# The last chain passes of 35 weight tiles carry the tile's scale, and two sums of token halves go to GpSimd

## The chip, the cores and the metric

One core of a Trainium2 chip runs the kernel. The metric is device time in microseconds (us), the median of three runs.

## The reference

The input x has 2048 tokens (4 x 512) of 512 features. It is normalised over the features, and three terms are added: x itself, a convolution along the features whose kernel comes from a small state-space model (S4), and a gated feed-forward layer with 4-bit weights. Cut to what matters:

```
def dequant_nf4(q, absmax, shape):
    w = NF4_CODE[q.reshape(-1)]
    w = w.reshape(-1, BLOCK) * absmax[:, None]
    return w.reshape(shape)
...
g = jnp.einsum('bsh,mh->bsm', x, Wg)        # M = 1792, HD = 512
u = jnp.einsum('bsh,mh->bsm', x, Wu)
h = jax.nn.silu(g) * u
return jnp.einsum('bsm,hm->bsh', h, Wd)
...
xn = _layernorm(x, axis=-1)
x = x + _L0_attn_ref(xn, ...) + _L0_ffn_ref(xn, ...)
```

## The kernel before, in words

Nothing is scheduled by a tool: each engine has its instructions written out in order, and semaphores tie them together. All large products are computed with float16 operands, and for accuracy each operand is the sum of a high and a low half, so every product is three matmuls (high-high, high-low, low-high).

**Weights.** The 42 weight tiles ("units" u: 14 each of gate, up and down, 128x512) arrive as int32 codes. GpSimd makes a first clamp of the codes (`first_pass`, L846). ScalarE then runs six Prelu passes, three on a left and three on a right chain (`chain_pass`, L937, tags l0 to r2). VectorE joins the chains (`step` WHOLE, L1310) and multiplies by the block's absmax (`step` SCALED, L1314). The high half, scaled by a power of two that stands in the tile `sc`, is made by ScalarE for units 0 to 6 and by GpSimd for the 35 units from 7 on (`weight_hi`, L859); VectorE makes the low half (`weight_lo`, L1324). For gate tiles GpSimd also keeps a scaled float32 copy (`gate_copy`, L868).

**Products.** From weight row k = 3 on, gate and up products are blocked by a Strassen-like scheme with seven products in place of eight: they need sums of weight blocks (`up_sums`, `other_sums`, split into halves by `block_hi` L1058 on ScalarE and `block_lo` L1370 and L1373 on VectorE) and sums of token blocks. The token sums start from high plus low halves of the normalised, transposed tokens `xT`: `token_whole` (L1385, eight of them, two sets s of four), then `token_sum` (L1396), ScalarE's `token_hi` and VectorE's `token_lo` (L1401). Each row k is a "window" in which TensorE runs 14 such products (`blocked_product`, L2270, six matmuls each); ScalarE moves partial results between banks (`copy_m1` L1030, `copy_m5` L1034) and makes silu (L1021), VectorE adds them (`join`, L1413) and multiplies (`h_mul`, L1439). After the windows come the convolution (L2337) and the down projection (L2347, L2397).

**Order around the change.** On GpSimd: `first_pass` of a unit, then layernorm rows (`norm`, L750), `first_pass(8)`, seventeen tiny steps of an exponential (L760 to L776), then a loop over the units from 7 on with `first_pass(u + 2)`, `weight_hi(u)`, `gate_copy(u)`. On VectorE the two sums `token_whole(1, 2)` and `token_whole(1, 3)` follow `step(8, SCALED)`, and `weight_lo(7)` comes later, just ahead of the first blocked window's sums. On ScalarE each window runs the chain passes of two or three units in a fixed place between bank copies and silu, and `block_hi` of the next row last.

Of the kernel before, what the change touches and what calls it, by code (L numbers as in the profile page):

```python
# [6 lines left out]
P = 128  # L7
# [102 lines left out]
]  # L110
CHAIN_TOP, CHAIN_STEP = 0.15385548770427704, 0.5004680156707764
CHAIN_ORDER = ("l0", "r0", "l1", "r1", "l2", "r2")
SIDES_ORDER = ("l0", "l1", "l2", "r0", "r1", "r2")
# [107 lines left out]
def ffn_conv_kernel(nc, x, q_gate, q_up, q_down, am_gate, am_up, am_down, am_flat, s4_cols, vct, bp,  # L221
# [5 lines left out]
    with ExitStack() as ctx:  # L227
# [17 lines left out]
        ident_h = ident[:].bitcast(F16)  # L245
        sc = sb("sc", [P, 34], F32)
        ones = sb("ones", [3, P], F32)
# [179 lines left out]
        def scale_of(u):  # L427
            return s_w[2 if SEQ[u] >= GU else SEQ[u] % 2]

        def whole_of(u):  # L430
            if u in CHAINED:
                return acc[:, (u - CHAINED[0]) % 3, :]
            return acc_1[:, 2, :]
# [51 lines left out]
        wlo_done = sem("wlo_done")  # L485
        sc_done = sem("sc_done")
        mx_tp = sem("mx_tp")
        mx_bc = sem("mx_bc")
# [17 lines left out]
        whs_lo = sem("whs_lo")  # L506
        xb_done = [sem(f"xb_done{s}") for s in range(2)]
        xs_done = [sem(f"xs_done{s}") for s in range(2)]
        xs_hi = [sem(f"xs_hi{s}") for s in range(2)]
# [226 lines left out]
        def _(pool):  # L736
# [112 lines left out]
            def weight_hi(u):  # L849

                pool.wait_ge(dq_done, dq_after(u, SCALED))
                unit = SEQ[u]
                if unit < GU:
                    before = room_before(unit // 2)
                    if LAST_USE[before] is not None:
                        pool.wait_ge((gate_done, up_done)[unit % 2], WHOLE_COUNT[LAST_USE[before]])
                    for s in sides(before):
                        pool.wait_ge(m_done[s], m_at(s, before, (2, 4)[unit % 2]))
                pool.tensor_scalar(weight_of(u)[HI], whole_of(u), scale_of(u), None, ALU.mult).then_inc(phi_done, 1)  # L859

# [51 lines left out]
        def _(act):  # L912
# [10 lines left out]
            def chain_pass(u, j):  # L923
# [123 lines left out]
            def block_hi(k, part):  # L1047
# [5 lines left out]
                elif n >= 2:  # L1053
                    for s in sides(k - 2):
# [225 lines left out]
        def _(dve):  # L1280
            v = nc.vector

            def step(u, s):
# [8 lines left out]
                elif s == WHOLE:  # L1292
# [11 lines left out]
                    if before < GU and before // 2 in BLOCKED:  # L1304
# [3 lines left out]
                        else:  # L1308
                            dve.wait_ge(w_done, 4 * blocked(before // 2) + 2)
                    ins = v.scalar_tensor_tensor(whole, left, CHAIN_TOP if u in CHAINED else LEFT_TOP, right, ALU.min, ALU.add)  # L1310
                else:
                    dve.wait_ge(am_ld[u % 2], 32 * (u // 2 + 1))
                    dve.wait_ge(dq_done, dq_after(u, WHOLE))
                    ins = v.scalar_tensor_tensor(whole, whole, CHAIN_STEP if u in CHAINED else -LEFT_TOP, am[:, u % 2, :],  # L1314
                                                 ALU.add, ALU.mult)
                ins.then_inc(dq_done, 1)

            def weight_lo(u):
# [20 lines left out]
            def up_sums(k, u):  # L1339

                n = blocked(k)
                whole, scale = whole_of(u), scale_of(u)
                g_whole, w_sums = sums_room(k)
                if n:
# [4 lines left out]
                dve.wait_ge(g_done, n + 1)  # L1349
                v.scalar_tensor_tensor(w_sums[:, 2, :], whole[:, 0:FH], scale, g_whole[:, 0:FH],  # L1350
                                       ALU.mult, ALU.subtract).then_inc(w_done, 1)

            def other_sums(k):
# [3 lines left out]
                dve.wait_ge(w_done, 4 * n + 1)  # L1357
                v.scalar_tensor_tensor(w_sums[:, 1, :], w_sums[:, 0, :], s_w[1], g_whole[:, 0:FH],
                                       ALU.mult, ALU.subtract).then_inc(w_done, 1)
                dve.wait_ge(w_done, 4 * n + 3)  # L1360
                v.tensor_tensor(w_sums[:, 3, :], g_whole[:, FH:HD], w_sums[:, 1, :], ALU.subtract).then_inc(w_done, 1)

            def block_lo(k, part):
# [4 lines left out]
                hi, lo = (sums_split(k, first, last)[:, :, l].rearrange("p i f m -> p i (f m)") for l in (HI, LO))  # L1368
                if part == 0:
                    v.scalar_tensor_tensor(lo, w_sums[:, first:last, :], s_w[1], hi,  # L1370
                                           ALU.mult, ALU.subtract).then_inc(whs_lo, 1)
                else:
                    v.tensor_tensor(lo, w_sums[:, first:last, :], hi, ALU.subtract).then_inc(whs_lo, 1)  # L1373

            def token_whole(s, i):

                c, f = (ROLE_E, ROLE_B)[i % 2][s], 2 * (i // 2)
                if s == 0 and f == 0:
                    dve.wait_ge(xt_ld[c - 2], 16 * TPC)
                elif s == 1 and i == 2:  # L1380
                    dve.wait_ge(xp_done, NT - POOL_NORMS)
                elif s == 1 and i == 0:
# [5 lines left out]
            def token_sum(s, i):  # L1388

                b12, b11, b22, b21 = x_sums[s]  # L1390
                if i == 0:
                    dve.wait_ge(xb_done[s], 4)
                else:
# [1077 lines left out]
```

## Time and profile before

| | |
|---|---|
| median of 3 runs | 455.39 us (454.79 to 456.29) |
| the profiled execution, its own time | 455.8 us |
| its span from the first to the last instruction | 454.0 us |
| TensorE busy | 439.6 us, 97% |
| VectorE busy | 397.2 us, 87% |
| ScalarE busy | 279.4 us, 62% |
| GpSimd busy | 214.7 us, 47% |
| mean granted TensorE clock | 0.996 |

The busy times overlap, so they don't add up to the span. TensorE's busy time is modelled from pipelined matmuls; whether it runs without holes is better read from when its products start.

### The profile page before, as it was taken

The page shows a single profiled execution, that of the slowest core. Times are in us where ns is not written, and L with a number is a line of the kernel's source. Part 1 is how long each engine was busy: PE and PEld are TensorE (multiplying, and loading weights), DVE is VectorE, ACT ScalarE, POOL GpSimd, SP SyncE. Part 2 cuts the span into 40 slices and gives each one's busy share as a digit, 9 for nine tenths or more (in the row PEclk, how much of TensorE's full clock was granted, in tenths as well). Part 3 has the DMA queues.
Part 4 walks back from the last instruction along what each step waited for, and adds up shares of the span by engine and source line. Part 5 has one row for each costly group of instructions (what it writes and reads, how often), then busy time and mean ns, then how long its engine had stood idle before and what let it go on. Part 6 is the DMA issues. An engine that isn't in the chain of part 4 may idle for free.

```text
span 454.0 us, 7272 instructions
## 1 busy us (share of the span) xinstructions
PE 439.6 (97%) x2560; PEld 251.6 (55%) x2560; DVE 397.2 (87%) x641; ACT 279.4 (62%) x472; POOL 214.7 (47%) x163
## 2 busy tenths in 40 slices
PE   1989999999999999999999999999999999999997
PEld 1744444444444444444444444466444788888886
DVE  5988979969889798999997779879996999999993
ACT  7878594395887859778675686855032643445340
POOL 2776299544956849769547757687100000000000
PEclk9989999999999999999999999999999999999999
DMA  8534636031415416336212243268790021101111
GB/s 301 163 131 145 157 71 176 1 92 46 164 48 185 162 48 208 113 120 209 71 47 71 60 126 78 86 212 252 212 361 31 17 79 48 46 1 48 48 48 46
DMA packets 34168, 51.41 MB, mean 113 GB/s; under 512 B 13076, under 2 KB 14164, under 8 KB 33364
## 3 DMA queue, kind: packets, MB, share of 16 engines
q1 hardware_dynamic: 34132, 50.95, 35.8%
q8 instruction: 20, 0.33, 0.3%
q14 instruction: 16, 0.13, 0.1%
HBM read 38.03 MB, written 10.81 MB: 108 GB/s over the span
## 4 chain that ended last, share of the span: by engine, by line
PE 91%; DVE 4%; DMA 2%; ACT 1%; issue 1%; POOL 1%; SPq 0%; DVEq 0%; POOLq 0%; ACTq 0%
PE bank L2270 38%; PE bank L2397 21%; PE bank L2115 17%; PE bank L2347 8%; PE bank L2337 6%; DMA h<-in_x 1%; DMA work<-in_q_gate 1%; PE bank L2151 0%; DVE work L1310 0%; DVE work L1314 0%; DVE at_s L1800 0%; POOL h L846 0%; PE bank L2207 0%; ACT xT L1096 0%; DVE w L1324 0%
## 5 line engine op out<-in xcount | busy, mean ns | idle before, releaser
L937 ACT ACTIVATE work<-work 128x512 f32<-128x512 f32 (+1 forms) x234 | 129.9, 625 | 11.5 <-POOL work L846 8.0
L846 POOL TENSOR_SCALAR work<-work 128x512 f32<-128x512 int32 x39 | 83.6, 2143 | 63.0 <-DVE work L1310 42.3
L2270 PE MATMUL bank<-h 128*128 128x512 f16 x360 | 81.4, 379 | 0.0
L2115 PE MATMUL bank<-xT,w 128*128 128x512 f16 (+1 forms) x300 | 66.2, 378 | 0.4 <-ACT yv L1124 0.4
L2270 PEld LDWEIGHTS bank<-h 128*128 128x128 f16 x360 | 35.1, 98 | 42.7 <-ACT bank L1030 0.7
L2397 PE MATMUL bank<-wd,work 128*128 128x256 f16 x504 | 56.2, 273 | 0.0
L2270 PE MATMUL bank<-xT,w 128*128 128x512 f16 x240 | 55.4, 379 | 0.0
L2397 PEld LDWEIGHTS bank<-wd,work 128*128 128x128 f16 (+1 forms) x504 | 49.3, 98 | 6.0
L2115 PEld LDWEIGHTS bank<-xT,w 128*128 128x128 f16 x300 | 30.0, 100 | 34.2 <-issue 1.6
L859 POOL TENSOR_SCALAR w<-work,sc 128x512 f16<-128x512 f32 x21 | 43.6, 2077 | 6.0 <-DVE work L1314 5.0
L1251 ACT ACTIVATE work<-h 128x896 f16<-128x896 f32 x30 | 27.9, 943 | 28.4 <-DVE h L2023 18.3
L2397 PE MATMUL bank<-h,work 128*128 128x256 f16 x378 | 42.2, 273 | 0.0
L2397 PEld LDWEIGHTS bank<-h,work 128*128 128x128 f16 x378 | 37.0, 98 | 4.3
L2270 PEld LDWEIGHTS bank<-xT,w 128*128 128x128 f16 x240 | 23.4, 98 | 28.1
L2347 PE MATMUL bank<-wd,h 128*128 128x512 f16 x168 | 36.4, 379 | 0.0
L2009 DVE TENSOR_TENSOR work<-h,work 128x896 bf16<-128x896 f32 x30 | 32.5, 1083 | 0.1
L1310 DVE SCALAR_TENSOR_TENSOR work<-work 128x512 f32<-128x512 f32 x39 | 27.5, 705 | 4.8 <-ACT work L937 4.8
L1021 ACT ACTIVATE work<-bank,sc 128x512 f32<-128x512 f32 x36 | 24.5, 681 | 10.8 <-PE bank L2115 10.8
L1314 DVE SCALAR_TENSOR_TENSOR work<-work 128x512 f32<-128x512 f32 x41 | 29.3, 714 | 1.1
L2270 PE MATMUL bank<-xT,h 128*128 128x512 f16 x120 | 27.9, 379 | 0.2 <-DVE bank L1413 0.2
L2270 PE MATMUL bank<-h,w 128*128 128x512 f16 x120 | 27.8, 379 | 0.0
L859 POOL TENSOR_SCALAR wd<-work,sc 128x512 f16<-128x512 f32 x14 | 25.5, 1821 | 4.5 <-PE bank L2337 2.5
(181 smaller groups left out, 659.7 us busy)
## 6 DMA issues: line engine op xcount, KB each, us to landing
moved<-h SPq DMA_DIRECT2D x6, 1024.0 KB, 4.9
h<-moved SPq DMA_DIRECT2D x4, 1536.0 KB, 16.5
h<-in_x SPq DMA_DIRECT2D x8, 512.0 KB, 5.2
xT<-in_x SPq DMA_DIRECT2D x16, 256.0 KB, 3.4
out<-xT SPq DMA_DIRECT2D x15, 256.0 KB, 2.1
work<-in_q_gate SPq DMA_DIRECT2D x14, 256.0 KB, 3.7
work<-in_q_up SPq DMA_DIRECT2D x14, 256.0 KB, 2.8
work<-in_am_gate SPq DMA_DIRECT2D x28, 128.0 KB, 3.0
```

Of the source, the lines that this page charges most:

```text
L846: pool.tensor_scalar(chain_room(u, "r"), qs[:, u % 2, :], RIGHT_FROM, RIGHT_FROM, ALU.max, ALU.subtract).then_inc(first_done, 1)
L859: pool.tensor_scalar(weight_of(u)[HI], whole_of(u), scale_of(u), None, ALU.mult).then_inc(phi_done, 1)
L937: nc.scalar.activation(room, qs[:, u % 2, :] if j == 0 else room, KNEE, scale=scale, bias=bias, alpha=below).then_inc(knee_done, 1)
L1251: nc.scalar.activation(slot_of(o)[:, HI], src, ACT.Copy).then_inc(o_hi, 1)
L1310: ins = v.scalar_tensor_tensor(whole, left, CHAIN_TOP if u in CHAINED else LEFT_TOP, right, ALU.min, ALU.add)
L1314: ins = v.scalar_tensor_tensor(whole, whole, CHAIN_STEP if u in CHAINED else -LEFT_TOP, am[:, u % 2, :], ALU.add, ALU.mult)
L2009: v.tensor_tensor(slot[:, LO].bitcast(BF16), src, slot[:, HI], ALU.subtract).then_inc(o_lo, 1)
L2115: mm = nc.tensor.matmul(out_b, weights(k)[:, unit, wl, f, :], xT[:, TPC * c + first:TPC * c + last, xl, f, :], start=(i == 0), stop=(i == ...
L2270: mm = nc.tensor.matmul(out_b, weight(wl, f), token(xl, f), start=(n == 0 and i in (1, 5)), stop=(n == 5), skip_group_check=i not in (1, 5))
L2337: mm = nc.tensor.matmul(bank[(t + 4) % 8][:, P * j:HD], xT[:, t, xl, j, :], tz[:, tl, 0:HD - P * j], start=(n == 0), stop=(n == 3 * NC - 1))
L2347: mm = nc.tensor.matmul(bank[(t + 4) % 8][:], part, wd[:, mt, wl, :], start=(mt == 0 and n == 0), stop=(mt == NM - 1 and n == 2))
L2397: mm = nc.tensor.matmul(out_b, part, w, start=(n == 0), stop=(n == 3 * KT - 1))
```

## The change

The scale of a unit from 7 on is no longer applied where the high half is made. It is folded into the constants of the chain: GpSimd computes six small rows once (`fold`, products of the three scales with six constants, into 18 new columns of `sc`). The last left pass and the last right pass on ScalarE then read scale and bias from `sc` instead of immediates, and the two steps on VectorE read their added constant from `sc`. Since the whole weight is then already scaled, `weight_hi` and `gate_copy` on GpSimd become plain copies, and `weight_lo`, the weight sums and `block_hi` part 0 lose their scale operand. Apart from that, `token_whole(1, 2)` and `token_whole(1, 3)` leave VectorE and are made by GpSimd, each as two instructions of 512 elements, behind the exponential's steps.

```diff
@@ gpsimd
-                pool.tensor_scalar(weight_of(u)[HI], whole_of(u), scale_of(u), None, ALU.mult).then_inc(phi_done, 1)
+                pool.tensor_copy(weight_of(u)[HI], whole_of(u)).then_inc(phi_done, 1)
...
-                pool.tensor_scalar(sums_room(SEQ[u] // 2)[0], whole_of(u), scale_of(u), None, ALU.mult).then_inc(g_done, 1)
+                pool.tensor_copy(sums_room(SEQ[u] // 2)[0], whole_of(u)).then_inc(g_done, 1)
+
+            def fold(i):
+
+                pool.wait_ge(sc_done, WEIGHT_SCALES)
+                pool.tensor_scalar(sc[:, 34 + 3 * i:37 + 3 * i], sc[:, 9:12], FOLDED[i], None, ALU.mult).then_inc(fold_done, 1)
+
+            def token_whole(i):
+
+                c = (ROLE_E, ROLE_B)[i % 2][1]
+                if i == 2:
+                    pool.wait_ge(xlo_done, NT)
...
+                hi, lo = (xT[:, TPC * c:TPC * c + TPC, l, 2:4, :] for l in (HI, LO))
+                made = x_sums[1][i].rearrange("p (f t m) -> p t f m", f=2, t=TPC)
+                for f in range(2):
+                    ins = pool.tensor_tensor(made[:, :, f], hi[:, :, f], lo[:, :, f], ALU.add)
+                ins.then_inc(xbp_done, 1)
...
             first_pass(7)
+            for i in range(len(FOLDED)):
+                fold(i)
...
             for i in range(EXP_STEPS):
                 exp_step(i)
+            token_whole(2)
+            token_whole(3)
@@ scalar
                 scale, bias, below = (RIGHT_CHAIN if side == "r" else LEFT_CHAIN)[i]
+                if u in POOL_HALVES and i == 2:
+                    act.wait_ge(fold_done, len(FOLDED))
+                    at = FOLD_RIGHT if side == "r" else FOLD_LEFT
+                    scale, bias = folded(u, at), folded(u, at + 1)
...
-                                     w_sums[:, first:last, :], ACT.Copy,
-                                     scale=1.0 if part else s_w[1]).then_inc(whs_hi, 1)
+                                     w_sums[:, first:last, :], ACT.Copy).then_inc(whs_hi, 1)
@@ vector
-                    ins = v.scalar_tensor_tensor(whole, left, CHAIN_TOP if u in CHAINED else LEFT_TOP, right, ALU.min, ALU.add)
+                    top = folded(u, FOLD_TOP) if u in POOL_HALVES else CHAIN_TOP if u in CHAINED else LEFT_TOP
...
+                    ins = v.scalar_tensor_tensor(whole, left, top, right, ALU.min, ALU.add)
...
-                v.scalar_tensor_tensor(lo, whole_of(u), scale_of(u), hi, ALU.mult, ALU.subtract).then_inc(wlo_done, 1)
+                if u in POOL_HALVES:
+                    v.tensor_tensor(lo, whole_of(u), hi, ALU.subtract).then_inc(wlo_done, 1)
...
-                v.scalar_tensor_tensor(w_sums[:, 1, :], w_sums[:, 0, :], s_w[1], g_whole[:, 0:FH],
-                                       ALU.mult, ALU.subtract).then_inc(w_done, 1)
+                v.tensor_tensor(w_sums[:, 1, :], w_sums[:, 0, :], g_whole[:, 0:FH], ALU.subtract).then_inc(w_done, 1)
...
             step(8, SCALED)
-            token_whole(1, 2)
-            token_whole(1, 3)
             h_mul(7)
```

Two places of the program's order matter. The first is GpSimd's queue between the layernorm rows and the first high half that it makes. Before, the last exponential step (L776) was followed at once by `first_pass(9)` (L846) and `weight_hi(7)` (L859):

```order
L846 TENSOR_SCALAR work<-work 128x512
L750 TENSOR_SCALAR h<-h 128x512 x4
L846 TENSOR_SCALAR work<-work 128x512
L772 TENSOR_SCALAR sc<-sc 128x1 x9
L774 TENSOR_SCALAR sc<-sc 128x1
L776 TENSOR_TENSOR sc<-sc 128x1
L846 TENSOR_SCALAR work<-work 128x512
L859 TENSOR_SCALAR w<-work,sc 128x512
L846 TENSOR_SCALAR work<-work 128x512
```

In the changed kernel (its lines are numbered some ten higher: `first_pass` is L856, `norm` L760, the exponential ends at L786, `weight_hi` is L869) the same stretch reads:

```order
L856 TENSOR_SCALAR work<-work 128x512
L883 TENSOR_SCALAR sc<-sc 128x3 x6
L760 TENSOR_SCALAR h<-h 128x512 x4
L856 TENSOR_SCALAR work<-work 128x512
L782 TENSOR_SCALAR sc<-sc 128x1 x9
L784 TENSOR_SCALAR sc<-sc 128x1
L786 TENSOR_TENSOR sc<-sc 128x1
L898 TENSOR_TENSOR h<-xT 128x512 x4
L856 TENSOR_SCALAR work<-work 128x512
L869 CAST w<-work 128x512
L856 TENSOR_SCALAR work<-work 128x512
```

The six folds (L883) stand ahead of four layernorm rows, and four additions of tokens (L898) stand between the exponential and `first_pass(9)`, so `weight_hi(7)` has four more instructions ahead of it. The second place is VectorE's queue around unit 8, where two of six `token_whole` groups (L1385) stood right behind `step(8, SCALED)` (L1314). Before:

```order
L1554 TENSOR_TENSOR h<-h 128x512 x4
L1310 SCALAR_TENSOR_TENSOR work<-work 128x512
L1314 SCALAR_TENSOR_TENSOR work<-work 128x512
L1385 TENSOR_TENSOR h<-xT 128x4x2x128 x2
L1439 SCALAR_TENSOR_TENSOR h<-bank,sc,work 128x512
L1385 TENSOR_TENSOR h<-xT 128x4x2x128 x2
L1396 TENSOR_TENSOR h<-h 128x1024
```

And in the changed kernel, where the steps are L1351 and L1356, `token_whole` is L1422, `h_mul` L1478 and `token_sum` L1435:

```order
L1593 TENSOR_TENSOR h<-h 128x512 x4
L1351 SCALAR_TENSOR_TENSOR work<-work,sc 128x512
L1356 SCALAR_TENSOR_TENSOR work<-work,sc 128x512
L1478 SCALAR_TENSOR_TENSOR h<-bank,sc,work 128x512
L1422 TENSOR_TENSOR h<-xT 128x4x2x128 x2
L1435 TENSOR_TENSOR h<-h 128x1024
```

The two steps now read `sc` as well, and `h_mul(7)` moves up by two instructions of 1024 elements.

## Rows read from the trace of the kernel before

**Rows 1.** The page, section 1: busy time, share of the span, instructions

```profile
PE 439.6 (97%) x2560; PEld 251.6 (55%) x2560; DVE 397.2 (87%) x641; ACT 279.4 (62%) x472; POOL 214.7 (47%) x163
```

**Rows 2.** Busy time by stretch: from:to, length, then engines; PEclk last but two

```profile
32.27:451.35 419.08, 418.87 (x2457) 237.54 (x2457) 371.94 (x568) 254.67 (x426) 196.85 (x143) 1.00 0.35 107
```

**Rows 3.** The chain that ended last, in order: start us, us, what

```profile
32.27 57.15 PE bank L2115 x264
...
355.03 96.30 PE bank L2397 x882
```

**Rows 4.** TensorE's waits: line, releaser, us in total, times, longest

```profile
PE bank L2141 <- DVE h L1459: 9.3, 1, 9.3
...
PE bank L2270 <- DVE bank L1413: 0.2, 1, 0.2
```

**Rows 5.** Groups on GpSimd: count, busy us, mean ns of one, idle before

```profile
L859 POOL TENSOR_SCALAR w<-work,sc 128x512 f16<-128x512 f32 x21 | 43.6, 2077 | 6.0 <-DVE work L1314 5.0
L859 POOL TENSOR_SCALAR wd<-work,sc 128x512 f16<-128x512 f32 x14 | 25.5, 1821 | 4.5 <-PE bank L2337 2.5 <-DVE work L1314 1.0
L868 POOL TENSOR_SCALAR h<-work,sc 128x512 f32<-128x512 f32 x10 | 16.2, 1617 | 6.9 <-DVE h L1361 6.9
L750 POOL TENSOR_SCALAR h<-h 128x512 f32<-128x512 f32 x15 | 16.0, 1081 | 11.0 <-DVE h L1545 10.9
...
L828 POOL CAST h<-work 128x512 f16<-128x512 f32 x9 | 6.6, 729 | 0.8 <-DVE work L1439 0.3
```

**Rows 6.** Groups on VectorE

```profile
L1310 DVE SCALAR_TENSOR_TENSOR work<-work 128x512 f32<-128x512 f32 x39 | 27.5, 705 | 4.8 <-ACT work L937 4.8
L1324 DVE SCALAR_TENSOR_TENSOR w<-work,sc,w 128x512 f16<-128x512 f32 x25 | 22.4, 898 | 1.7 <-POOL w L859 1.4 <-ACT w L964 0.3
L1439 DVE SCALAR_TENSOR_TENSOR h<-h,sc,work 128x512 f32<-128x512 f32 x20 | 15.4, 773 | 1.9
...
L1385 DVE TENSOR_TENSOR h<-xT 128x1024 f32<-128x1024 f16 x8 | 10.0, 1266 | 0.0
...
L1370 DVE SCALAR_TENSOR_TENSOR h<-h,sc 128x256 f16<-128x256 f32 x11 | 5.3, 486 | 4.2 <-ACT h L1058 4.2
...
L1554 DVE TENSOR_TENSOR h<-h 128x512 f16<-128x512 f32 x8 | 5.1, 692 | 0.0
```

**Rows 7.** Groups on ScalarE

```profile
L937 ACT ACTIVATE work<-work 128x512 f32<-128x512 f32 x195 | 109.4, 625 | 8.5 <-POOL work L846 8.0
...
L964 ACT ACTIVATE w<-work,sc 128x512 f16<-128x512 f32 x4 | 2.9, 716 | 3.1 <-DVE work L1314 3.1
...
L1072 ACT ACTIVATE h<-h 128x512 f32<-128x512 f32 x1 | 0.8, 812 | 0.5 <-DVE h L1545 0.5
```

**Rows 8.** GpSimd in order of time: start us, us, what, [idle before]

```profile
54.96 1.68 POOL L750 TENSOR_SCALAR h<-h 128x512 f32<-128x512 f32 x1 [8.16 <-DVE h L1545]
...
75.52 2.81 POOL L846 TENSOR_SCALAR work<-work 128x512 f32<-128x512 int32 x1
78.42 2.24 POOL L859 TENSOR_SCALAR w<-work,sc 128x512 f16<-128x512 f32 x1
```

**Rows 9.** In order of time, ahead of the first blocked sums' product

```profile
87.56 0.74 DVE L1324 SCALAR_TENSOR_TENSOR w<-work,sc,w 128x512 f16<-128x512 f32 x1
...
91.60 0.58 DVE L1370 SCALAR_TENSOR_TENSOR h<-h,sc 128x256 f16<-128x256 f32 x1
...
93.15 0.81 PE L2270 MATMUL bank<-h 128*128 128x512 f16 x3
```

**Rows 10.** In order of time, the end of one window: ScalarE, VectorE, TensorE

```profile
177.63 0.53 ACT L1058 ACTIVATE h<-h,sc 128x256 f16<-128x256 f32 x1
...
178.20 0.48 DVE L1370 SCALAR_TENSOR_TENSOR h<-h,sc 128x256 f16<-128x256 f32 x1 [1.17 <-ACT h L1058]
...
180.40 0.68 DVE L1413 TENSOR_TENSOR h<-bank,h 128x512 f32<-128x512 f32 x1
...
179.96 2.75 PE L2270 MATMUL bank<-h,w 128*128 128x512 f16 x12
```

More of the change, by code:

```diff
@@ L111 @@
 CHAIN_TOP, CHAIN_STEP = 0.15385548770427704, 0.5004680156707764
+FOLDED = (LEFT_CHAIN[2][0], LEFT_CHAIN[2][1], RIGHT_CHAIN[2][0], RIGHT_CHAIN[2][1], CHAIN_TOP, CHAIN_STEP)
+FOLD_LEFT, FOLD_RIGHT, FOLD_TOP, FOLD_STEP = 0, 2, 4, 5
 CHAIN_ORDER = ("l0", "r0", "l1", "r1", "l2", "r2")
@@ L245, in ffn_conv_kernel @@
         ident_h = ident[:].bitcast(F16)
-        sc = sb("sc", [P, 34], F32)
+        sc = sb("sc", [P, 34 + 3 * len(FOLDED)], F32)
         ones = sb("ones", [3, P], F32)
@@ L428, in scale_of, with folded @@
             return s_w[2 if SEQ[u] >= GU else SEQ[u] % 2]
+        def folded(u, i):
+            at = 34 + 3 * i + (2 if SEQ[u] >= GU else SEQ[u] % 2)
+            return sc[:, at:at + 1]
         def whole_of(u):
@@ L486, in ffn_conv_kernel @@
         sc_done = sem("sc_done")
+        fold_done = sem("fold_done")
         mx_tp = sem("mx_tp")
@@ L507, in ffn_conv_kernel @@
         xb_done = [sem(f"xb_done{s}") for s in range(2)]
+        xbp_done = sem("xbp_done")
         xs_done = [sem(f"xs_done{s}") for s in range(2)]
@@ L867, in gate_copy @@
                 pool.wait_ge(w_done, 4 * blocked(SEQ[u] // 2))
-                pool.tensor_scalar(sums_room(SEQ[u] // 2)[0], whole_of(u), scale_of(u), None, ALU.mult).then_inc(g_done, 1)
+                pool.tensor_copy(sums_room(SEQ[u] // 2)[0], whole_of(u)).then_inc(g_done, 1)
[6 more added lines that the diff above has]
+                    pool.wait_ge(xlo_done, NT)
+                    pool.wait_ge(xn_done, POOL_NORMS)
+                    pool.wait_ge(xp_done, NT - POOL_NORMS)
+                    pool.wait_ge(rs_step, RSTD * NCH)
+                    pool.wait_ge(sc_done, 13)
+                    pool.wait_ge(b_mm, 1)
+                hi, lo = (xT[:, TPC * c:TPC * c + TPC, l, 2:4, :] for l in (HI, LO))
[3 more added lines that the diff above has]
+                ins.then_inc(xbp_done, 1)
             first_pass(1)
@@ L1309, in step @@
                             dve.wait_ge(w_done, 4 * blocked(before // 2) + 2)
-                    ins = v.scalar_tensor_tensor(whole, left, CHAIN_TOP if u in CHAINED else LEFT_TOP, right, ALU.min, ALU.add)
+                    top = folded(u, FOLD_TOP) if u in POOL_HALVES else CHAIN_TOP if u in CHAINED else LEFT_TOP
+                    if u == POOL_HALVES[0]:
+                        dve.wait_ge(fold_done, len(FOLDED))
+                    ins = v.scalar_tensor_tensor(whole, left, top, right, ALU.min, ALU.add)
                 else:
@@ L1313, in step @@
                     dve.wait_ge(dq_done, dq_after(u, WHOLE))
-                    ins = v.scalar_tensor_tensor(whole, whole, CHAIN_STEP if u in CHAINED else -LEFT_TOP, am[:, u % 2, :],
+                    step_up = folded(u, FOLD_STEP) if u in POOL_HALVES else CHAIN_STEP if u in CHAINED else -LEFT_TOP
+                    ins = v.scalar_tensor_tensor(whole, whole, step_up, am[:, u % 2, :],
                                                  ALU.add, ALU.mult)
@@ L1323, in weight_lo @@
                 hi, lo = weight_of(u)
-                v.scalar_tensor_tensor(lo, whole_of(u), scale_of(u), hi, ALU.mult, ALU.subtract).then_inc(wlo_done, 1)
+                if u in POOL_HALVES:
+                    v.tensor_tensor(lo, whole_of(u), hi, ALU.subtract).then_inc(wlo_done, 1)
+                else:
+                    v.scalar_tensor_tensor(lo, whole_of(u), scale_of(u), hi, ALU.mult, ALU.subtract).then_inc(wlo_done, 1)
             def items(first, last):
@@ L1341, in up_sums @@
                 n = blocked(k)
-                whole, scale = whole_of(u), scale_of(u)
+                whole = whole_of(u)
                 g_whole, w_sums = sums_room(k)
@@ L1349, in up_sums @@
                 dve.wait_ge(g_done, n + 1)
-                v.scalar_tensor_tensor(w_sums[:, 2, :], whole[:, 0:FH], scale, g_whole[:, 0:FH],
-                                       ALU.mult, ALU.subtract).then_inc(w_done, 1)
+                v.tensor_tensor(w_sums[:, 2, :], whole[:, 0:FH], g_whole[:, 0:FH], ALU.subtract).then_inc(w_done, 1)
             def other_sums(k):
@@ L1357, in other_sums @@
                 dve.wait_ge(w_done, 4 * n + 1)
-                v.scalar_tensor_tensor(w_sums[:, 1, :], w_sums[:, 0, :], s_w[1], g_whole[:, 0:FH],
-                                       ALU.mult, ALU.subtract).then_inc(w_done, 1)
+                v.tensor_tensor(w_sums[:, 1, :], w_sums[:, 0, :], g_whole[:, 0:FH], ALU.subtract).then_inc(w_done, 1)
                 dve.wait_ge(w_done, 4 * n + 3)
@@ L1368, in block_lo @@
                 hi, lo = (sums_split(k, first, last)[:, :, l].rearrange("p i f m -> p i (f m)") for l in (HI, LO))
[L1369 to L1373, printed above, removed]
+                v.tensor_tensor(lo, w_sums[:, first:last, :], hi, ALU.subtract).then_inc(whs_lo, 1)
             def token_whole(s, i):
@@ L1379, in token_whole @@
                     dve.wait_ge(xt_ld[c - 2], 16 * TPC)
-                elif s == 1 and i == 2:
-                    dve.wait_ge(xp_done, NT - POOL_NORMS)
                 elif s == 1 and i == 0:
@@ L1391, in token_sum @@
                 if i == 0:
-                    dve.wait_ge(xb_done[s], 4)
+                    dve.wait_ge(xb_done[s], 4 if s == 0 else 2)
+                    if s == 1:
+                        dve.wait_ge(xbp_done, 2)
                 else:
```

## The prediction

> **What bounds the kernel now.** I began with the page's busy shares. TensorE stands at 97%, VectorE at 87%, ScalarE at 62% and GpSimd at 47% [rows 1]. A modelled busy time proves little, so I read next the chain that ended last. Over its length it is TensorE's: from 32.27 us on, one piece of 57.15 us with 264 matmuls of 512 columns, which is 0.2165 us for each, and at the end 882 matmuls of 256 columns in 96.30 us, 0.109 us each [rows 3]. The time for one column is thus 0.42 ns in both, which is what 2.4 GHz gives, and the granted clock is 1.00 of that from 32.27 to 451.35 us [rows 2]. Third, TensorE's own waits: 9.3 us before the first matmul, and in the long middle a single hole of 0.2 us, a product that waited for a `join` on VectorE [rows 4]. In the 419.08 us from 32.27 on TensorE shows 418.87 us busy [rows 2]. So TensorE sets the end, the other engines only feed it, and what they save is worth nothing unless a hole closes. The opening up to 32.27 us does have holes, but nothing in it is changed: the first changed instruction is the fold on GpSimd, behind `first_pass(7)`, in the idle time that ends at 54.96 us [rows 8].
>
> The question is therefore whether the change opens new holes. I went to the two kinds of place where TensorE's operands arrive with little to spare: the first sums of row 3 (one time only), and the joins at the end of each window.
>
> **Part 1, GpSimd's copies.** 21 high halves took 2.077 us and 14 took 1.821 us, 10 copies 1.617 us. The nearest row to a plain copy is the cast of the same shape, 0.729 us [rows 5]. That saves 21 x 1.35 + 14 x 1.09 + 10 x 0.89 = 52.5 us of GpSimd, of 214.7. All of it lies beside TensorE. VectorE waited 1.4 us for the `w` halves [rows 6] and ScalarE 8.0 us for `first_pass` [rows 7], so both get their input somewhat sooner. On the end: 0, or up to the 0.2 us of the hole.
>
> **Part 2, VectorE's operands.** 70 steps read a constant from `sc`. A step with an immediate takes 0.705 us, `h_mul` with such a scalar 0.773 us [rows 6]: at most +0.07 each, +4.9 us. 35 low halves go from 0.898 us (the `w` group; I take it for all) to the 0.692 us of a plain subtraction [rows 6]: -7.2 us. The small sums change by less than 0.1 us each. Two of eight token sums leave, 1.266 us each [rows 6]: -2.5 us. Together about -5 us of 397, spread over the run.
>
> **Part 3, ScalarE's last passes.** This is the part that adds. A pass with immediates takes 0.625 us, the copy with a scale from `sc` 0.716 us, and the one instruction with both scale and bias in memory 0.812 us [rows 7]. A folded pass is nearest to the last: +0.187 us, and there are 2 x 35: +13.1 us of ScalarE, 279 becoming about 292. The bounds are 0 and 0.19 each. `block_hi` part 0 loses its scale (-0.09, eleven times).
> The Trainium skill, ScalarE: Activation LUTs, under "What ACT_TABLE_LOAD costs", says the same against this change: each operand of one value per partition adds about 93 ns. By it the sum would be 70 x 0.186 = 13.0 us, and rows 7 agree with it (0.716 and 0.812 against 0.625).
> Is it hidden? Where ScalarE waits for TensorE or VectorE between its groups, yes. Where a window's passes run without a pause, `block_hi` comes later, and the join behind it. Over eleven low halves (L1370) VectorE waited 4.2 us for `block_hi` [rows 6], so it is the later one in a part of the windows. The tightest such window ends so: `block_hi` starts at 177.63, VectorE has idled 1.17 us for it at 178.20, then joins, the second at 180.40 for 0.68 us, ending 181.08. TensorE's twelve matmuls start at 179.96, so the second product of six starts at 179.96 + 6 x 0.216 = 181.26 [rows 10]. That is 0.18 us to spare. Four folded passes stand ahead of this `block_hi` without a pause: 4 x 0.187 - 0.09 = +0.66 us. Less 0.18, a new hole of 0.5 us. In the windows where VectorE is the later one, ScalarE's extra time fits in front of it, or GpSimd's sooner first pass pays it back. I count one such hole.
>
> **Part 4, folds.** Six instructions of 3 columns. Taken as dear as a whole layernorm row, 1.081 us [rows 5], six are 6.5 us, inside the 8.16 us for which GpSimd idled until 54.96 [rows 8]. Cost 0; without that cover, up to 6.5 us ahead of layernorm rows of the last token block.
>
> **Part 5, token sums on GpSimd.** Four additions of 512 elements with two inputs. No row shows a wide one. Lower bound 0.729 us, the cast with one input; upper 2.81 us, the `first_pass` at 75.52, made while VectorE was busy as well [rows 5, 8]. Two input streams at the cast's price are 1.46 us, and this stretch holds GpSimd up, so I take 1.9: 7.6 us. Queued behind them are `first_pass(9)`, `weight_hi(7)`, and VectorE's `weight_lo(7)`, which ran at 87.56. `weight_hi(7)` ended at 78.42 + 2.24 = 80.66 [rows 8]; now 80.66 + 7.6 - (2.24 - 0.73) = 86.75, which is 0.8 us before VectorE asks. Behind that the chain ends with `block_lo` at 91.60 + 0.58 = 92.18, and TensorE's product needs it at 93.15 [rows 9], another 0.97 us. Hidden, with 1.8 us to spare in all.
> The Trainium skill, GPSIMD Engine Reference, "3.1 Elementwise", has 4.497 us for a two-input add of 2048 elements. An estimate from it is 4 x 1.12 = 4.5 us, with which the sums would be hidden more easily; no row here shows it.
>
> **The sum.** Profiled time 455.8 us, a span of 454.0 and 1.8 around it. Holes: +0.5 (part 3), -0.2 (part 1), 0 for the rest: 456.1. The median of the runs shown is 0.4 below the profiled execution, so 455.7 as a median; since freed VectorE time eases that same join by a little, I say **455.6**.
>
> **The rivals.**
> *ScalarE becomes the feeder in every blocked window.* There are nine windows with both sets (rows k = 5 to 13), and if each loses what the tightest loses, 0.5 to 0.66 us, it is 4.5 to 5.9 us: about 460.6. For it: the price per pass is in the rows, and a hole moves TensorE but not the number of passes. Against it: ScalarE was busy 254.67 us of 419.08 [rows 2], and VectorE waited only 4.2 us for `block_hi` over all windows [rows 6]. It decides against me from three such windows on (1.5 us). Chance 0.07.
> *GpSimd is late with unit 7.* The holes start when an addition costs more than (0.97 + 6.90 + 1.51) / 4 = 2.35 us, where 6.90 is 87.56 - 80.66. At 2.81 us it is 4 x 0.46 = 1.9 us: 457.5. For it: GpSimd and VectorE slow each other in this stretch (`first_pass` 2.81 us there). Against it: VectorE itself has 2.5 us less to do there, and it is one place only. Chance 0.05.
> *The relief is real.* If the joins, sums and halves come sooner everywhere, the 0.2 us hole closes, no new one opens: 455.2. This is a part of "no change", chance 0.25 beside 0.58 for the forecast proper. For a gain over 0.3% (1.4 us) more holes would have to close than the 419.08 - 418.87 = 0.21 us [rows 2] that there are; only a luckier opening could give it, about 453.9. Chance 0.05.
>
> **How the numbers follow.** Over 0.3%, 1.4 us, is about what a measurement of this kernel can tell from no change. No change: 0.58 + 0.25 = 0.83. Slower: 0.07 + 0.05 = 0.12. Faster: 0.05. The range leaves out the 460.6 and the 453.9: below, the relief case with the scatter of the runs shown (0.6 under their median) gives 454.6, rounded down to 454.3 for the opening; above, the forecast with two more holes of 0.5 us and 0.3 of scatter gives 456.9, and the late unit 7 lies partly within.
>
> **What would show it.** Right: the folded passes appear as a form of some 0.81 us; GpSimd's high halves near 0.73 us and its busy time near 170 us; VectorE near 392 us; TensorE's pieces in the chain as long as before, its waits after 32 us under 1 us. At the end of the window of rows 10, a wait for `join` of about half a microsecond. Wrong: a wait of TensorE for `join` or `block_lo` in most windows (first rival), or a wait near 93 us behind `weight_lo(7)` or `block_lo` (second). It would also be wrong if copies on GpSimd held up VectorE more than the multiplications did.

## The result, and the profile after

| | before | after |
|---|---|---|
| median of the runs, us | 455.63 (4 runs, 454.79 to 456.29) | 457.75 (4 runs, 457.37 to 458.27) |
| ratio after to before | | 1.0041, interval 1.0026 to 1.0056 |
| profiled execution, us | 455.8 | 457.37 |
| its span, us | 454.0 | 455.6 |

The changed kernel is slower by 0.4%. That is above the forecast of 455.6 us and above its range, which ended at 456.9 us.

From the page of the kernel after, its busy times and the shares of the engines in the chain that ended last:

```profile
PE 437.7 (96%) x2560; PEld 249.1 (55%) x2560; DVE 398.4 (87%) x639; ACT 290.4 (64%) x472; POOL 172.6 (38%) x173
...
PE 79%; DVE 12%; issue 3%; ACT 2%; DMA 2%; SPq 1%; POOL 1%; DVEq 0%; ACTq 0%; POOLq 0%
```

GpSimd fell from 214.7 us to 172.6 and ScalarE rose from 279.4 to 290.4, much as forecast. VectorE did not fall: 397.2 to 398.4 [rows 1]. In the chain VectorE has 12% now. Before, the same line of the page was:

```profile
PE 91%; DVE 4%; DMA 2%; ACT 1%; issue 1%; POOL 1%; SPq 0%; DVEq 0%; POOLq 0%; ACTq 0%
```

So TensorE probably waited for VectorE somewhere. Its waits say where. These are TensorE's waits after (who waits, for whom, us in total, times, longest), and behind them its rows by time around 90 us:

```profile
PE bank L2178 <- DVE h L1498: 8.8, 1, 8.8
...
PE bank L2307 <- DVE h L1412: 1.0, 1, 1.0
...
PE bank L2152 <- DVE w L1367: 0.6, 1, 0.6
```

```profile
91.17 2.76 PE L2152 MATMUL bank<-xT,w 128*128 128x512 f16 x12 [0.57 <-DVE w L1367]
94.90 2.32 PE L2307 MATMUL bank<-h 128*128 128x512 f16 x10 [0.97 <-DVE h L1412]
```

The 8.8 us stand ahead of the first matmul, where before had 9.3 [rows 4]; the lines left out are waits of the opening, which ended no later than before (32.15 us, before 32.27). The other two are new: 0.57 us for `weight_lo(7)` (L1367 now), 0.97 us for `block_lo` part 0 (L1412 now). They are nearly all that TensorE lacks from 32.15 us on, 418.85 less 417.30 us, 1.55 us, in this row of the windows (from:to, length, busy time of TensorE first), where before lacked 0.21 [rows 2]:

```profile
32.15:451.00 418.85, 417.30 (x2442) 236.02 (x2443) 372.19 (x566) 265.94 (x426) 154.76 (x153) 1.00 0.34 106
```

The product behind the second hole started at 94.90 us, before at 93.15 [rows 9]: 1.75 us later, though the steady run began 0.12 us sooner. The span grew by 1.6 us. So the loss is made at this one place; what is lost and won after it comes to 0.2 us or less.

Why was VectorE late there? The next two fences are VectorE and GpSimd after, by time: start, us, engine, line and operation, count, and the idle time ahead in brackets.

```profile
70.72 3.32 DVE L1422 TENSOR_TENSOR h<-xT 128x1024 f32<-128x1024 f16 x2 [1.06 <-DMA xT<-h]
74.07 2.07 DVE L1435 TENSOR_TENSOR h<-h 128x1024 f32<-128x1024 f32 x1
...
76.72 3.61 DVE L1435 TENSOR_TENSOR h<-h 128x1024 f32<-128x1024 f32 x2
80.25 1.62 DVE L1422 TENSOR_TENSOR h<-xT 128x1024 f32<-128x1024 f16 x1
...
90.43 0.68 DVE L1367 TENSOR_TENSOR w<-work,w 128x512 f16<-128x512 f32 x1
...
94.29 1.43 DVE L1412 TENSOR_TENSOR h<-h 128x256 f16<-128x256 f32 x2
```

```profile
65.94 4.19 POOL L782 TENSOR_SCALAR sc<-sc 128x1 f32<-128x1 f32 x9
...
70.73 8.52 POOL L898 TENSOR_TENSOR h<-xT 128x512 f32<-128x512 f16 x4
79.34 2.79 POOL L856 TENSOR_SCALAR work<-work 128x512 f32<-128x512 int32 x1
82.19 0.61 POOL L869 CAST w<-work 128x512 f16<-128x512 f32 x1
```

And the same two engines before, first VectorE, then GpSimd:

```profile
68.20 2.35 DVE L1385 TENSOR_TENSOR h<-xT 128x1024 f32<-128x1024 f16 x2
...
71.14 2.35 DVE L1385 TENSOR_TENSOR h<-xT 128x1024 f32<-128x1024 f16 x2
73.52 1.22 DVE L1396 TENSOR_TENSOR h<-h 128x1024 f32<-128x1024 f32 x1
...
75.32 2.76 DVE L1396 TENSOR_TENSOR h<-h 128x1024 f32<-128x1024 f32 x2
```

```profile
65.68 9.19 POOL L772 TENSOR_SCALAR sc<-sc 128x1 f32<-128x1 f32 x9
```

Three things are to be seen.

First, the two sums that left VectorE stood at 68.20 to 70.55 us. What comes behind them needs tokens that a transfer brings, and after the change VectorE idles for it until 70.72. It starts its next sums 0.42 us sooner than before, not the 2.4 us of the work that was taken away.

Second, GpSimd's four additions (L898) run from 70.73 to 79.25, beside VectorE's sums. One takes 2.13 us (8.52 / 4). VectorE's sums took 2.35 us for two, 1.22 for one and 2.76 for two before; the same now take 3.32, 2.07 and 3.61. The wait at the tokens gone, the same row of work from the token sums to `weight_lo(7)` took 90.43 - 70.72 = 19.71 us instead of 87.56 - 71.14 = 16.42: 3.29 us held up. Less the 0.42 us, `weight_lo(7)` came 2.87 us later.

This lateness accounts for the loss: `block_lo` part 0 came at 94.29 us, before at 91.60, 2.69 us later. It had 0.97 us to spare [rows 9], which leaves 1.72, and the product behind it started 1.75 us later.

Third, `weight_hi(7)` ended at 82.80 us, and VectorE asked for it only at 90.43. GpSimd was not late at all, by 7.6 us.

### The profile page after: what moved, and what is told of

It is laid out like the page before. It is cut to its first block, busy times and chain, and to the rows that moved or that the text cites. A ratio compares the mean times of both kernels' runs of the same rounds, so it can differ in the third digit from the quotient of the medians.

```text
span 455.6 us, 7354 instructions
## 1 busy us (share of the span) xinstructions
PE 437.7 (96%) x2560; PEld 249.1 (55%) x2560; DVE 398.4 (87%) x639; ACT 290.4 (64%) x472; POOL 172.6 (38%) x173
## 4 chain that ended last, share of the span: by engine, by line
PE 79%; DVE 12%; issue 3%; ACT 2%; DMA 2%; SPq 1%; POOL 1%; DVEq 0%; ACTq 0%; POOLq 0%
PE bank L2307 40%; PE bank L2434 21%; PE bank L2384 8%; PE bank L2374 6%; PE bank L2152 3%; DVE h L1422 2%; DVE h L1539 1%; ACT work L976 1%; DMA work<-in_q_gate 1%; DVE h L1440 1%; DVE h L1593 1%; DVE work L1351 1%; DVE h L1478 1%; DVE work L1356 1%; DMA xT<-h 1%
## 5 line engine op out<-in xcount | busy, mean ns | idle before, releaser
L856 POOL TENSOR_SCALAR work<-work 128x512 f32<-128x512 int32 x39 | 82.0, 2104 | 95.7 <-DVE work L1351 77.8
L976 ACT ACTIVATE work<-work 128x512 f32<-128x512 f32 (+1 forms) x164 | 93.0, 625 | 8.4 <-POOL work L856 6.6
L976 ACT ACTIVATE work<-work,sc 128x512 f32<-128x512 f32 x70 | 53.0, 809 | 0.0
L1351 DVE SCALAR_TENSOR_TENSOR work<-work,sc 128x512 f32<-128x512 f32 x35 | 27.7, 791 | 4.9 <-ACT work L976 4.9
L1356 DVE SCALAR_TENSOR_TENSOR work<-work,sc 128x512 f32<-128x512 f32 x35 | 27.9, 796 | 0.9
L2384 PEld LDWEIGHTS bank<-wd,h 128*128 128x128 f16 x168 | 16.4, 98 | 19.6
```

The lines of the kernel that those rows point to most:

```text
L856: pool.tensor_scalar(chain_room(u, "r"), qs[:, u % 2, :], RIGHT_FROM, RIGHT_FROM, ALU.max, ALU.subtract).then_inc(first_done, 1)
L1351: ins = v.scalar_tensor_tensor(whole, left, top, right, ALU.min, ALU.add)
L1356: ins = v.scalar_tensor_tensor(whole, whole, step_up, am[:, u % 2, :], ALU.add, ALU.mult)
L2384: mm = nc.tensor.matmul(bank[(t + 4) % 8][:], part, wd[:, mt, wl, :], start=(mt == 0 and n == 0), stop=(mt == NM - 1 and n == 2))
```

## The experiments

The theory from the two traces: **GpSimd's additions and VectorE's sums both read from SBUF, the core's on-chip memory, and hold each other up, so VectorE is late with the first blocked window**. The rivals: the scale's fold has a part in it; the additions lengthen GpSimd's own queue, which is what counts; or the place of the two sums on VectorE mattered in itself. Each kernel is measured against the kernel before on the same chip. The lines of each kernel are numbered a little differently; names of steps are those of the text ahead.

| kernel | median, us | runs | ratio to before | interval |
|---|---|---|---|---|
| fold_only | 455.71 | 12 | 1.0002 | 0.9987 to 1.0017 |
| tokens_only | 457.58 | 12 | 1.0037 | 1.0021 to 1.0053 |
| tokens_sooner | 458.97 | 6 | 1.0070 | 1.0045 to 1.0094 |
| sums_left_out | 455.60 | 12 | 0.9997 | 0.9982 to 1.0012 |
| one_input | 459.18 | 7 | 1.0058 | 1.0037 to 1.0079 |
| sums_twice | 461.11 | 4 | 1.0099 | 1.0071 to 1.0126 |
| exp_later | 455.68 | 12 | 0.9988 | 0.9972 to 1.0004 |
| tokens_later | 455.68 | 12 | 0.9988 | 0.9971 to 1.0004 |

The medians of the kernel before were 455.94 us beside the first four and 455.84 us beside the last four. The ratios are those on record, and they differ from the quotients of these medians by up to 0.0017.

### fold_only and tokens_only: each half of the change alone

fold_only is the changed kernel with all eight token sums back on VectorE:

```diff
-            token_whole(2)
-            token_whole(3)
...
+            token_whole(1, 2)
+            token_whole(1, 3)
```

> The scale folded as in the changed kernel, but all eight token sums stay on VectorE. If GpSimd's two-input additions are what holds VectorE up between 70 and 80 us (my theory now), the two holes of TensorE near 91 and 95 us (1.9 us together) are gone and the time is that of before, 455.6 us within 0.8. If ScalarE's dearer passes (0.809 us in place of 0.625) are the cause, the time stays near 457.7 us and the holes show at the joins of the windows. I expect the passes to cost no more than 0.3 us in holes, since before had two holes there that close.

Measured: 1.0002. Among TensorE's waits there is none for `weight_lo`, `block_lo` or `join`. In time, folding the scale costs nothing and gives nothing that could be measured. It does use up room: in fold_only VectorE begins `step(8, WHOLE)` at 67.69 us, before at 66.78, and `block_lo` part 0 ends at 92.92 us, with TensorE's product at 93.16. Of the 0.97 us to spare 0.24 are left.

tokens_only is the kernel before with nothing but the two sums moved:

```diff
+            token_whole(2)
+            token_whole(3)
...
-            token_whole(1, 2)
-            token_whole(1, 3)
```

> The kernel of before with the one part alone that two token sums are made by GpSimd; the scale stays where it was. If the additions on GpSimd are the cause, the time is 457 to 458.5 us, with TensorE's holes near 91 and 95 us; here weight_hi(7) is the dear one (2.1 us in place of 0.61), which ends near 84.5 us and still does not matter. If the fold is the cause, 455.6 us.

Measured: 1.0037, against 1.0041 for the whole change; the intervals lie over each other. TensorE's rows by time show the same two holes, the first one shorter:

```profile
91.31 2.76 PE L2132 MATMUL bank<-xT,w 128*128 128x512 f16 x12 [0.24 <-DVE w L1343]
95.28 1.89 PE L2287 MATMUL bank<-h 128*128 128x512 f16 x8 [1.21 <-DVE h L1389]
```

The loss comes with the two sums.

### sums_left_out: what is it worth to free VectorE of them?

GpSimd fills the room of the two sums with zeros and reads nothing; this part of the computation, two of the eight sums of high and low halves, is left out. VectorE's program is that of the changed kernel, so the place of its own instructions is the same.

```diff
-                for f in range(2):
-                    ins = pool.tensor_tensor(made[:, :, f], hi[:, :, f], lo[:, :, f], ALU.add)
-                ins.then_inc(xbp_done, 1)
+                pool.memset(x_sums[1][i], 0.0).then_inc(xbp_done, 1)
```

> The changed kernel in which nobody makes the two token sums: GpSimd fills their room with zeros by one short instruction each, so this kernel leaves out a part of the computation. It tells what taking them off VectorE is worth when nobody pays. By the trace VectorE then waits for the tokens of block 3 at 70.7 us anyway, so I expect the time of fold_only within 0.5 us, 455.4 us, with no hole near 91 us. If VectorE's load there had been a limit, it would be lower by up to the 2.5 us of the two sums, but TensorE has no such holes to close.

Measured: 0.9997. GpSimd and VectorE by time:

```profile
70.66 1.84 POOL L895 MEMSET h<- 128x1024 f32 x2
```

```profile
70.65 2.36 DVE L1418 TENSOR_TENSOR h<-xT 128x1024 f32<-128x1024 f16 x2 [1.03 <-DMA xT<-h]
73.04 1.22 DVE L1431 TENSOR_TENSOR h<-h 128x1024 f32<-128x1024 f32 x1
...
87.09 0.68 DVE L1363 TENSOR_TENSOR w<-work,w 128x512 f16<-128x512 f32 x1
```

Two results. Even for free, the move is worth nothing in time: `weight_lo(7)` at 87.09 instead of 87.56 us feeds a TensorE that had no hole there. With VectorE's order unchanged and the holes gone, that order was not the cause either. And GpSimd instructions that only write, started in the same 0.01 us as VectorE's sums, left those at 2.36 us for two.

### tokens_sooner: the additions ahead of the exponential

In the changed kernel GpSimd's seventeen steps of the exponential run from 61.9 to 70.7 us, ahead of VectorE's sums, and the additions beside them. Here the two change places:

```diff
-            for i in range(EXP_STEPS):
-                exp_step(i)
             token_whole(2)
             token_whole(3)
+            for i in range(EXP_STEPS):
+                exp_step(i)
```

> The changed kernel with the seventeen steps of the exponential moved behind the two token sums on GpSimd, so that the four additions run from about 65.3 to 74 us in place of 70.7 to 79.2, partly while VectorE idles for codes and tokens. If it is the overlap with VectorE's sums that costs, only the additions after 70.7 us hurt (about 1.5 of 4): the holes shrink from 1.9 to 0.5 us or less, 456.2 us. If instead VectorE loses by having GpSimd at work at all, or by the lateness of first_pass(9) and weight_hi(7), nothing is gained: 457.7 us.

Measured: 1.0070, a miss: no gain, and if anything worse than the change. A part of the reason behind the expectation held. GpSimd by time, then VectorE:

```profile
65.58 5.39 POOL L898 TENSOR_TENSOR h<-xT 128x512 f32<-128x512 f16 x4 [3.55 <-DVE h L1593]
...
77.80 9.48 POOL L782 TENSOR_SCALAR sc<-sc 128x1 f32<-128x1 f32 x9
...
89.93 0.61 POOL L869 CAST w<-work 128x512 f16<-128x512 f32 x1
```

```profile
68.50 1.46 DVE L1356 SCALAR_TENSOR_TENSOR work<-work,sc 128x512 f32<-128x512 f32 x1
...
70.97 2.36 DVE L1422 TENSOR_TENSOR h<-xT 128x1024 f32<-128x1024 f16 x2 [0.35 <-DMA xT<-h]
...
90.58 0.69 DVE L1367 TENSOR_TENSOR w<-work,w 128x512 f16<-128x512 f32 x1 [4.14 <-POOL w L869]
```

The additions took 5.39 us in place of 8.52, and VectorE's sums 2.36 for two, as before. They still met one of VectorE's instructions, `step(8, SCALED)`, which took 1.46 us where the changed kernel has 0.76; but that stands ahead of the wait for the tokens, which fell from 1.06 to 0.35 us and so took up the delay. What I had not reckoned with: the seventeen tiny steps now lay beside VectorE's sums, and these hold up GpSimd's steps as well. Nine of them took 9.48 us; in the changed kernel, where they run ahead of VectorE's sums, the same nine took 4.19 us. So `weight_hi(7)` ended at 90.54 us, and VectorE stood 4.14 us for it. Here, and only here, GpSimd is late with unit 7.

### one_input and sums_twice: what on GpSimd holds VectorE up, and does it scale?

Two readings were left: that both instructions must have two inputs, or that any GpSimd instruction that reads SBUF is enough. one_input replaces each of the four additions by three copies of the high halves, with one input each; the low halves are left out of these two sums.

```diff
-                for f in range(2):
-                    ins = pool.tensor_tensor(made[:, :, f], hi[:, :, f], lo[:, :, f], ALU.add)
+                for again in range(3):
+                    for f in range(2):
...
+                        ins = pool.tensor_copy(made[:, :, f], hi[:, :, f])
```

> The changed kernel with each two-input addition on GpSimd replaced by three copies of one input (high halves alone, so the two token sums lack their low halves), twelve copies of 0.6 to 0.7 us in about the time of the four additions of 2.13 us. Theory A: what holds VectorE up is that GpSimd works on two inputs of SBUF while VectorE's instruction has two inputs too; then with one input on GpSimd VectorE's sums stay near 1.3 us, the holes near 91 and 95 us are under 0.7 us in sum, and the time is 456.0 us. Theory B: any reading by GpSimd holds up a two-input instruction of VectorE; then its sums again take 1.5 to 2.2 us, and the time is 457 to 458 us.

Measured: 1.0058. The sums are as theory B has them; the time, 459.18 us, is above its 457 to 458. TensorE waited 1.3 us for `weight_lo(7)` and 1.4 us for `block_lo`. GpSimd and VectorE by time (the whole stretch stands some 1.7 us later than in the kernel after):

```profile
72.33 15.37 POOL L902 CAST h<-xT 128x512 f32<-128x512 f16 x12
```

```profile
72.40 3.17 DVE L1428 TENSOR_TENSOR h<-xT 128x1024 f32<-128x1024 f16 x2 [1.14 <-DMA xT<-h]
...
77.70 3.19 DVE L1441 TENSOR_TENSOR h<-h 128x1024 f32<-128x1024 f32 x2
...
92.25 1.09 DVE L1373 TENSOR_TENSOR w<-work,w 128x512 f16<-128x512 f32 x1
```

Copies with one input hold VectorE up: 3.17 us for two sums in place of 2.36. From the sums' start to `weight_lo(7)` it is 92.25 - 72.40 = 19.85 us, against 16.42 before. That is 3.43 us for twelve copies, 0.29 us each. The reading that GpSimd needs two inputs for it is gone.

sums_twice makes each addition twice, eight in all, with the same inputs and the same output:

```diff
+                for again in range(2):
+                    for f in range(2):
...
+                            ins = pool.tensor_tensor(made[:, :, f], hi[:, :, f], lo[:, :, f], ALU.add)
```

> The changed kernel with each of the two token sums made twice on GpSimd: eight additions in place of four, from 70.7 to about 88 us. Each addition cost VectorE about 0.9 us where both engines had two inputs, so VectorE's chain to the first block sums should be 3 to 4 us later than in the changed kernel, and weight_hi(7) comes at about 91 us, now late as well: 460 to 462 us. If the holes had another cause than the additions, the time stays at 457.7 us.

Measured: 1.0099, 461.11 us, as expected. VectorE by time:

```profile
71.94 4.32 DVE L1428 TENSOR_TENSOR h<-xT 128x1024 f32<-128x1024 f16 x2 [1.08 <-DMA xT<-h]
...
94.26 0.68 DVE L1373 TENSOR_TENSOR w<-work,w 128x512 f16<-128x512 f32 x1
```

From the sums' start to `weight_lo(7)` 22.32 us: 16.42 with none of the additions, 19.71 with four, 22.32 with eight. Each addition costs VectorE 0.82 us over the four and 0.74 us over the eight.

### exp_later and tokens_later: the same work, apart in time

If the overlap is the cause, then moving the work where the two don't meet must bring back the time of before, with all of the change kept. exp_later makes the additions at 66 us, and the exponential (nobody needs it soon) behind `weight_hi(8)`:

```diff
-            for i in range(EXP_STEPS):
-                exp_step(i)
             token_whole(2)
             token_whole(3)
...
+                if u == 8:
+                    for i in range(EXP_STEPS):
+                        exp_step(i)
```

> The changed kernel with the additions at about 65.5 us and the exponential's seventeen steps behind weight_hi(8), so that neither VectorE's sums after 71 us nor weight_hi(7) are held up. In the kernel with the additions sooner they took 1.16 to 1.60 us each and VectorE's sums 1.22 us, but the steps, held up by VectorE, made weight_hi(7) late (90.6 us). If that account is right, weight_hi(7) ends near 79 us, both holes are gone and the time is that of before, 455.6 us. If GpSimd's lateness moves on to gate_copy(8), a hole of up to 1 us near 100 us stays.

Measured: 0.9988 (0.9972 to 1.0004). VectorE by time:

```profile
71.81 2.36 DVE L1423 TENSOR_TENSOR h<-xT 128x1024 f32<-128x1024 f16 x2 [0.34 <-DMA xT<-h]
...
88.25 0.68 DVE L1368 TENSOR_TENSOR w<-work,w 128x512 f16<-128x512 f32 x1
```

16.44 us from the sums to `weight_lo(7)`, as before (16.42), and TensorE has no wait for VectorE there.

tokens_later moves the two sums into the loop over the units instead, one behind `gate_copy` of unit 8 and one a round later:

```diff
-            token_whole(2)
-            token_whole(3)
...
+                if u in (8, 9):
+                    token_whole(u - 6)
```

> The changed kernel with the two token sums made one each behind gate_copy(8) and weight_hi(9), from about 92 us on, where VectorE has pauses and nobody needs them before 104.5 us. If it is the overlap with VectorE's chain of 71 to 92 us that costs, both holes are gone: 455.6 us, unless the second sum comes too late for the token sum at 104.5 us, which would cost a hole of under 1 us later, 456.3 us. If GpSimd's additions cost their hold-up wherever they stand, 457.5 us.

Measured: 0.9988 (0.9971 to 1.0004). GpSimd and VectorE by time:

```profile
90.83 3.15 POOL L898 TENSOR_TENSOR h<-xT 128x512 f32<-128x512 f16 x2
```

```profile
86.81 0.68 DVE L1367 TENSOR_TENSOR w<-work,w 128x512 f16<-128x512 f32 x1
...
90.67 2.29 DVE L1412 TENSOR_TENSOR h<-h 128x256 f16<-128x256 f32 x2
```

The first pair of additions runs behind `weight_lo(7)`. It still meets VectorE (3.15 us for two), and `block_lo` takes 2.29 us in all where the changed kernel has 1.43. But part 0, which TensorE needs at 92.44 us, is done at 91.14 in its usual 0.47 us; it is part 1 that is held up. Both kernels have the fold and GpSimd's sums and lose nothing. Neither is measurably faster than the kernel before: from 32 us on TensorE had only 0.21 us of holes [rows 2].

## Why the prediction was wrong

**The step that failed** is Part 5, with its conclusion "Hidden, with 1.8 us to spare in all". It followed one queue, GpSimd's, and asked when `weight_hi(7)` would end. There it came out 3.95 us too late: 82.80 us measured where 86.75 was worked out. The additions were dearer by 0.9 us in all, but they began 4.8 us sooner, because the exponential's steps no longer lay beside two of VectorE's sums; the prediction had not counted that. That error was on the safe side. The one that mattered is that it set GpSimd's time against VectorE's times of before, held fixed at 87.56 and 91.60 us, and these moved by 2.87 and 2.69 us. Of the 1.8 us to spare, 0.8 lay between GpSimd and VectorE and could cushion only a late GpSimd; against a late VectorE there were 0.97 us, as worked out, and the rest became the loss.

**The price of one addition** was about right as a length: 1.9 us taken, 2.13 measured. The runs show what it is made of: 5.39 / 4 = 1.35 us where few of VectorE's instructions are in the way (the first two 1.16 each), 2.13 beside its sums. What was missing is the other half of the same account. "This stretch holds GpSimd up" was read from the rows of before. The second rival even says that the two engines slow each other there, but neither it nor Part 5 puts a price on VectorE's side: 3.29 us over the four.

**"VectorE itself has 2.5 us less to do there"** stood against the second rival, and this too was wrong. The work went (2.35 us), but its place was ahead of a wait for the tokens' transfer; the gain behind it was 0.42 us, and with zeros in place of the sums (sums_left_out) it was worth nothing to the end.

**The rivals.** The second one, "GpSimd is late with unit 7", named the place (near 93 us) and the time, 457.5, against 457.75 measured. Its mechanism did not happen: VectorE did not wait for `weight_hi(7)`. In tokens_sooner it did, held up by the exponential's steps and not by dear additions. Its chance was 0.05, and no rival had the mechanism that decided, so that its time came so near is luck. ScalarE as the feeder did not come about, as fold_only shows.

**Part 1** held in its sum, 172.6 us of GpSimd where 170 was forecast, and partly by luck. The copies saved 50.1 us and not 52.5, since a high half takes 0.830 us and not 0.729; the folds and the dearer additions added to it; and the exponential's nine steps gave back 5.0 us that nobody had counted.

**Part 2** was mis-sized in both directions. Steps and low halves after, groups on VectorE:

```profile
L1356 DVE SCALAR_TENSOR_TENSOR work<-work,sc 128x512 f32<-128x512 f32 x35 | 27.9, 796 | 0.9
L1351 DVE SCALAR_TENSOR_TENSOR work<-work,sc 128x512 f32<-128x512 f32 x35 | 27.7, 791 | 4.9 <-ACT work L976 4.9
...
L1367 DVE TENSOR_TENSOR w<-work,w 128x512 f16<-128x512 f32 x21 | 15.5, 738 | 0.0
```

A step costs 0.79 us, above the 0.773 given as its upper end; a low half 0.738 in this group and 0.769 in that of `wd`, not 0.692. fold_only, with no additions on GpSimd, has VectorE at 396.4 us where before has 397.2 [rows 1]: by these two profiles the fold saves it 0.8 us, not 2.3. The two sums should then have taken another 2.5 us off; instead the changed kernel stands 2.0 us above fold_only, at 398.4. The fairest comparison is sums_left_out, with the same instructions on VectorE and no additions anywhere: 394.9 us. So the additions make VectorE's instructions 3.5 us longer, nearly all of it in the 3.29 us ahead of `weight_lo(7)`.

**Part 3** was right in its price and too high in its effect. The folded passes after:

```profile
L976 ACT ACTIVATE work<-work,sc 128x512 f32<-128x512 f32 x70 | 53.0, 809 | 0.0
```

0.809 us against 0.812 taken, and ScalarE at 290.4 us against 292. The hole at the end of the window of [rows 10] is there, but small. The same place after, ScalarE, VectorE and TensorE, and behind it one line of VectorE before:

```profile
180.17 1.16 ACT L1097 ACTIVATE h<-h 128x256 f16<-128x256 f32 x2
180.63 0.43 DVE L1412 TENSOR_TENSOR h<-h 128x256 f16<-128x256 f32 x1 [2.50 <-ACT h L1097]
...
181.76 0.75 DVE L1478 SCALAR_TENSOR_TENSOR h<-h,sc,work 128x512 f32<-128x512 f32 x1
181.81 2.91 PE L2307 MATMUL bank<-h,w 128*128 128x512 f16 x12
```

```profile
179.39 1.09 DVE L1439 SCALAR_TENSOR_TENSOR h<-h,sc,work 128x512 f32<-128x512 f32 x1
```

TensorE is 1.85 us later here than before and `block_hi` 2.54 us: 0.7 us more, as worked out. But VectorE made up for 0.34 us of it with an `h_mul` of 0.75 us in place of 1.09. Before, GpSimd's `gate_copy` of 1.56 us lay beside it; after, the plain copy of 0.61 us is over by then. TensorE's twelve matmuls take 2.91 us in place of 2.75, a hole of some 0.16 us and not 0.5. It does not stand among the waits of the view, and fold_only has it too, while tokens_only, without the fold, does not.

**Part 4** held. Six folds fitted into GpSimd's idle time, of which 5.79 us were left:

```profile
45.95 3.08 POOL L883 TENSOR_SCALAR sc<-sc 128x3 f32<-128x3 f32 x6
54.82 1.68 POOL L760 TENSOR_SCALAR h<-h 128x512 f32<-128x512 f32 x1 [5.79 <-DVE h L1584]
```

**The rule against this change.** What the traces show is a hold-up, in both directions, between VectorE's instructions with two inputs from SBUF and GpSimd's that read it: 3.32 us for two sums in place of 2.35, and 2.13 us for an addition in place of 1.35. The Trainium skill, SBUF — State Buffer, "Who interferes with whom", states just this: a VectorE instruction with two SBUF inputs contends with a GpSimd instruction that reads SBUF, not with one that only writes it. one_input (copies, VectorE 3.17 us for two) and sums_left_out (zeros, 2.36 us for two) agree with both halves of it. The prediction did not weigh it.

**What stays open.** What in the chip makes the two engines wait for each other the runs do not show, only who holds up whom and when. Nor do they show why `first_pass` in the same stretch, 2.81 us beside VectorE before [rows 8], cost VectorE less than an addition did: VectorE's two sums at 75.32 us took 2.76 us in all, only 0.41 us above the 2.35 of other pairs.

## What to carry to other kernels

Work moved from VectorE to GpSimd was not off VectorE here where VectorE read two operands from SBUF: each addition cost VectorE some 0.8 us. So price each GpSimd instruction in both queues, and look at what VectorE does in that very stretch. Ask next whether the work removed stood ahead of a wait, because then its time is not won. And when the engine that is fed has no holes (0.21 us here), such a move has next to nothing to win; its right place is one where the two engines don't meet ahead of a deadline.

## What the runs showed of the hardware that was not expected

Tiny GpSimd steps are held up too. Nine steps on 128 x 1 elements took 4.19 us in the changed kernel and 9.48 us beside VectorE's sums (tokens_sooner): 1.05 us each in place of 0.47, near the length of one of VectorE's sums, 1.2 us. In the kernel before they took 9.19 us, beside the two token sums at 68.20 us and the next two: taking these sums off VectorE gave GpSimd its 5 us back, and at once put its additions beside the sums that are left.

The steps hardly held VectorE up in turn. In tokens_sooner, from VectorE's sums at 70.97 us to `weight_lo(7)`, less the 4.14 us of waiting, it is 15.47 us, with only steps on GpSimd. That is 0.95 us less than the 16.42 of before, where `first_pass` and `weight_hi` lay in the stretch.

A one-input copy costs GpSimd 15.37 / 12 = 1.28 us beside VectorE's sums, and the cast at 82.19 us in the kernel after took 0.61 us. The high half with a scale from memory, 2.077 us before [rows 5], is a plain cast of 0.830 us after, shown in this group on GpSimd:

```profile
L869 POOL CAST w<-work 128x512 f16<-128x512 f32 x21 | 17.4, 830 | 7.4 <-DVE work L1356 6.7
```

A multiplication by one value per partition thus costs GpSimd more than twice the cast without it.
